# The node cell's candidate bias as a bf16 product over three rows, its state product 384 columns wide

## The reference, cut to what matters

```python
def _gru_cell(x, hstate, Wih, Whh, bih, bhh):
    gi = x @ Wih.T + bih
    gh = hstate @ Whh.T + bhh
    ir, iz, inn = jnp.split(gi, 3, axis=1)
    hr, hz, hn = jnp.split(gh, 3, axis=1)
    r = jax.nn.sigmoid(ir + hr)
    z = jax.nn.sigmoid(iz + hz)
    n = jnp.tanh(inn + r * hn)
    return (1.0 - z) * n + z * hstate
...
edge_output = _gru_cell(node_support, h, edge_Wih, edge_Whh, edge_bih, edge_bhh)
...
edge_support = edge_support / HEADS
node_output = _gru_cell(edge_support, h, node_Wih, node_Whh, node_bih, node_bhh)
return de[:, None] * edge_output + dn[:, None] * node_output
```

## Time and profile before

| | |
|---|---|
| median of 3 runs | 1427.51 us (1426.62 to 1429.61) |
| the profiled execution's own time | 1426.91 us |
| its span in the profile | 1425.2 us |
| TensorE busy | 1332.1 us, 93% |
| VectorE busy | 922.3 us, 65% |
| ScalarE busy | 554.7 us, 39% |
| GpSimd busy | 193.4 us, 14% |
| mean granted clock of TensorE | 0.977 |
| L1461, the state's product: 52 passes | 1361.7 to 1402.3 us |
| L1462, the input's product: 52 passes | 1362.7 to 1403.0 us |

### The profile page before, as it was taken

How to read it: one execution, slowest core, us unless ns; L and a number is a source line. 1 busy time by engine, 2 the same in 40 slices (tenths; PEclk the granted TensorE clock), 3 DMA queues, 4 the chain that set the end, 5 groups by cost and what they waited for, 6 DMA issues and landing times.

```text
span 1425.2 us, 11729 instructions
## 1 busy us (share of the span) xinstructions
PE 1332.1 (93%) x4294; PEld 677.7 (48%) x4294; DVE 922.3 (65%) x1277; ACT 554.7 (39%) x491; POOL 193.4 (14%) x211
## 2 busy tenths in 40 slices
PE   5889997899989999999999999999999999999993
PEld 4434444344444444455445455544445444544451
DVE  6978887888864000003225453799978987898576
ACT  7543324966730000000211111456565566455343
POOL 0000002000020000000000000225430233124211
PEclk8999997999999999999999999999999999999997
DMA  9899972000026667658667158698877987688301
GB/s 396 331 389 412 391 305 99 0 0 0 0 97 187 194 195 193 193 151 268 197 219 235 35 171 308 256 371 307 313 263 256 338 314 290 240 309 319 138 1 50
DMA packets 78150, 311.10 MB, mean 218 GB/s; under 512 B 8700, under 2 KB 20603, under 8 KB 61307
## 3 DMA queue, kind: packets, MB, share of 16 engines
q1 hardware_dynamic: 78075, 310.17, 61.2%
HBM read 306.71 MB, written 3.43 MB: 218 GB/s over the span
## 4 chain that ended last, share of the span: by engine, by line
PE 83%; DMA 7%; DVE 7%; ACT 2%; issue 1%; POOL 0%; ACTq 0%; DVEq 0%; POOLq 0%; SPq 0%
PE ps L1440 30%; PE ps L1241 10%; PE ps L1175 10%; PE ps L1278 10%; PE ps L1100 6%; DMA ring<-in_adjR 6%; PE ps L1235 5%; PE ps L1350 2%; PE ps L1461 1%; DVE arena L1560 1%; PE ps L1422 1%; PE ps L1259 1%; PE ps L1462 1%; DMA ring<-in_adjB 1%; PE ps L1215 1%; PE ps L1260 1%
## 5 line engine op out<-in xcount | busy, mean ns | idle before, releaser
L1440 PE MATMUL ps<-arena,x 128*128 128x512 f32 (+1 forms) x1092 | 438.9, 562 | 2.9 <-ACT shared L978 1.6
L1440 PEld LDWEIGHTS ps<-arena,x 128*128 128x128 f32 x1092 | 206.1, 190 | 231.4 <-issue 225.2
L971 ACT ACTIVATE arena<-arena,bench 128x3328 f32<-128x3328 bf16 x78 | 239.8, 3075 | 188.8 <-PE ps L1440 176.4
L2145 DVE TENSOR_TENSOR arena<-arena,ring 128x3328 f32<-128x3328 f32 x51 | 184.7, 3621 | 26.6 <-ACT arena L971 26.1
L1241 PE MATMUL ps<-ring,x 128*128 128x512 f32 (+1 forms) x364 | 176.1, 566 | 0.0
L1278 PE MATMUL ps<-ring,x 128*128 128x512 f32 (+1 forms) x364 | 149.5, 563 | 1.3 <-DMA ring<-in_adjB 1.3
L1100 PE MATMUL ps<-ring,bench 128*128 128x512 f32 x260 | 122.7, 607 | 15.0 <-DMA ring<-in_adjR 15.0
L1845 DVE SCALAR_TENSOR_TENSOR bench<-b,cols,ps 128x128 f32<-128x128 f32 x26 | 7.3, 344 | 182.1 <-PE ps L1215 182.1
L715 POOL TENSOR_TENSOR ring<-ring,nid 128x128 f32<-128x128 f32 x51 | 95.1, 1864 | 210.8 <-DMA ring<-in_adjR 210.8
L1235 PE MATMUL ps<-arena,shared 128*128 128x512 fp8e4 (+1 forms) x364 | 103.6, 366 | 6.1 <-DVE shared L1650 6.1
L2145 DVE TENSOR_TENSOR arena<-arena 128x3328 f32<-128x3328 f32 x27 | 98.0, 3631 | 13.5 <-ACT arena L971 13.1
(11 more groups left out here) (326 smaller groups left out, 1513.4 us busy)
## 6 DMA issues: line engine op xcount, KB each, us to landing
ring<-in_adjR SPq DMA_DIRECT2D x51, 1664.0 KB, 8.7
ring<-in_adjB SPq DMA_DIRECT2D x312, 256.0 KB, 3.0
arena<-in_adjR SPq DMA_DIRECT2D x27, 1664.0 KB, 8.8
ring<-in_adjR SPq DMA_DIRECT2D x25, 1280.0 KB, 8.5
shared<-in_adj SPq DMA_DIRECT2D x7, 1664.0 KB, 10.8
es<-in_adj SPq DMA_DIRECT2D x7, 1664.0 KB, 10.6
xT<-in_adj SPq DMA_DIRECT2D x6, 1664.0 KB, 13.3
y<-in_adj SPq DMA_DIRECT2D x6, 1664.0 KB, 13.1
```

Of the source, the lines that this page charges most:

```text
L971: A_(E[n % 3], below[n % 3], ACT.Exp, bias=tt_[:, t * HEADS + k:t * HEADS + k + 1], scale=-WIN).then_inc(e_exp, 1)
L1440: last = mm(ps[:, b, 0:w], lhsT=x[:, t], rhs=E[n % 3][:, o_:o_ + w], start=(t == 0), stop=(t == TILES - 1))
L2145: v.tensor_tensor(E[n % 3], E[n % 3], row_at(n), ALU.mult).then_inc(q_ready, 1)
```

## The change

In the node cell, the state's product becomes 384 columns wide, without the bias of inn. The input's product is split in two, 256 columns (r and z) and 128 (inn). Between them a new product opens inn: `ones16`, three rows of ones in bf16, as stationary operand, and `inn16`, whose three rows are the bias split into three bf16 numbers that add up to it. Both lie in the space of the former fourth part of the weights.

```diff
-        state_weights = gb[:, 1].rearrange("p a f -> p (a f)")
+        state_weights = gb[:, 1, 0:3].rearrange("p a f -> p (a f)")
+        inn_bias = gb[:, 1, 3]
+        inn16, ones16 = (inn_bias.bitcast(BF16)[:, n * F:(n + 1) * F] for n in range(2))
...
-                            mm(gt[:, 0:4 * F], lhsT=ht, rhs=state_weights, start=True, stop=False)
-                            last = mm(gt[:, F:4 * F], lhsT=ut, rhs=gru[:, 2], start=False, stop=True)
+                            mm(gt[:, 0:G3], lhsT=ht, rhs=state_weights, start=True, stop=False)
+                            mm(gt[:, F:G3], lhsT=ut, rhs=gru[:, 2, 0:2 * F], start=False, stop=True)
+
+                            mm(gt[:, G3:4 * F], lhsT=ones16[0:3, :], rhs=inn16[0:3, :], start=True, stop=False)
+                            last = mm(gt[:, G3:4 * F], lhsT=ut, rhs=gru[:, 2, 2 * F:], start=False, stop=True)
...
-                step(v.scalar_tensor_tensor(state_weights[:, 0:G3], state_weights[:, 0:G3], lone[:], gru[:, 3], ALU.mult, ALU.add))
-                step(v.tensor_scalar(state_weights[:, G3:], state_weights[:, G3:], lone[:], None, ALU.mult))
+                step(v.scalar_tensor_tensor(state_weights, state_weights, lone[:], gru[:, 3], ALU.mult, ALU.add))
+                first, second, rest, last = (stage[:, n // 2, n % 2 * P:n % 2 * P + P] for n in range(4))
+                first, second = (a.bitcast(BF16)[:, 0:P] for a in (first, second))
+                step(v.tensor_copy(first, inn_bias))
+                step(v.tensor_tensor(rest, inn_bias, first, ALU.subtract))
+                step(v.tensor_copy(second, rest))
+                step(v.tensor_tensor(last, rest, second, ALU.subtract))
+                step(v.tensor_scalar(inn16, first, ident[:, 0:1], None, ALU.mult))
+                step(v.scalar_tensor_tensor(inn16, second, ident[:, 1:2], inn16, ALU.mult, ALU.add))
+                step(v.scalar_tensor_tensor(inn16, last, ident[:, 2:3], inn16, ALU.mult, ALU.add))
+                step(v.tensor_copy(ones16, ones[:]))
...
-LATE_READY = 42
-GS_READY = 55
+LATE_READY = 49
+GS_READY = 62
...
-OUT_READY = 59
+OUT_READY = 66
```

## The result

| | before | changed |
|---|---|---|
| median of 7 runs | 1426.62 us (1424.99 to 1429.61) | 1431.54 us (1426.48 to 1433.73) |
| the profiled execution's own time | 1426.91 us | 1429.71 us |
| its span | 1425.2 us | 1427.9 us |

The ratio of the changed kernel to the one before is 1.003, with a 95% interval of 1.0018 to 1.0043: between 2.6 and 6.1 us longer. The forecast was 5.2 us longer.

A forecast was written before the change was run, and what follows sets the result against it. TensorE was taken to bound the node cell: a tile goes from 1.50 to 1.30 + 0.40 = 1.70 us, 26 tiles x 0.20 = 5.2 us longer, forecast 1432.4 us (between 1432.1 and 1432.7), range 1428.8 to 1435.2.

The forecast's parts named there:

- What bounds the stage: Node cell, last stage: TensorE alone sets the pace, 3.22 us a group of two tiles; VectorE's own period is 3.01 us.
- The three float32 products, 1.30 us: Node cell, each tile: products of 384, 256 and 128 columns take 1.30 us as in the edge cell, 0.20 less than 1.50.
- Two stops: Around the three-row bf16 product: its weight load and the next float32 load each start 0.09 us behind the stream ahead.
- The size of the bf16 product, 0.40 us: Node cell, between the 256 and 128 column products: the three-row product adds 0.40 us to each tile, both stops included.
- the forecast's own case: Node cell: both stops, at 0.37 to 0.50 us a tile, make the kernel 4.4 to 7.8 us longer; chance 0.77.
- All before 1361 us unmoved: Sign of a right forecast: everything ahead of the node cell's stage, before 1361 us, keeps its times.
- The set-up is hidden: VectorE's set-up at about 450 us: seven more steps, about 2.3 us, cost nothing under its 19.66 us wait for TensorE.
- Rival 1, no stop: Node cell: three-row product costs 0.12 us like a full one, group 3.06, 1.9 us shorter, 1425.3 us; chance 0.14.
- Rival 2, one stop: Node cell: way into the bf16 product hidden, price 0.25 to 0.30 us, 1.3 to 2.6 us longer, about 1429.5; chance 0.07.
- Rival 3, the clock: Node cell: VectorE or the clock as a new bound, with TensorE streaming 81% of the stage; the clock's chance 0.02.

## Why the prediction was right, point by point

- *What bounds the stage.* Right: TensorE, at 3.22 us a group, with VectorE close behind. The 3.01 us read for VectorE was 0.04 too long: without a bias product it does a group in 2.97. In the run with 128 rows both engines run at 3.04, TensorE's pace.
- *The three float32 products, 1.30 us.* Right: 1.30 in the run that has only them. The edge cell was a fair model, in spite of its other order.
- *Two stops.* Right, and now shown and not only read from two small products: 64 against 65 rows changes nothing else, and one float32 row has the stops without a change of type. Why the step lies between 64 and 65 rows is not shown. The signs named for it came too: the load 0.09 us behind the stream, and VectorE's wait at 0.47 us where about 0.55 was said.
- *The size of the bf16 product, 0.40 us.* Too large, and outside the 0.37 to 0.50 us to which the forecast gave 0.77. Measured it is 1.66 - 1.30 = 0.36, by the group (3.53 - 0.22) / 2 - 1.30 = 0.355. Way in 0.09 as said, exposed float32 load 0.11 as said; between them 0.155 where the sum had 0.20. If 0.09 of that is the way out, as with one float32 row, and 0.05 the stream (the pair of bf16 products shows 0.05 for one more), the bf16 load has only 0.01 to 0.02. The sum had 0.06 for it, near half a float32 load. The halves for a bf16 stream and a bf16 load were the author's estimate, which no row of before shows by itself; for the stream the runs agree with it, for the load they do not. A tile is thus 1.30 + 0.355 - 1.50 = 0.155 longer, and 26 of them are 4.0 us instead of 5.2.
- *The time.* The stage grew by 3.89 us, less than the 4.4 to 7.8 of the forecast's own case; the medians differ by 4.9, and the interval of the whole, 2.6 to 6.1 us, holds all of 3.9, 4.4 and 5.2. That the median, 1431.54, is within 0.9 us of 1432.4 is therefore luck in part. The lower bound was also worked out unevenly: one stop, 1.3 to 2.6 us longer, has its middle at 1429.2 from the 1427.2 that the forecast starts from, while 1428.8 counts from the profiled execution alone.
- *All before 1361 us unmoved.* Not so, by 1.12 us, but earlier and not later. It is no sign of the set-up: over the ten profiles the first transposes begin between 1358.94 us (the kernel before with the set-up's steps) and 1362.52 (no bias product).
- *The set-up is hidden.* Right, and shown by adding seven such steps alone.
- *Rival 1, no stop.* This is what the run with 128 rows is, with the 0.11 us by tile read off L1363. Its gain had been worked out as 1.9 us; the stage became 2.26 shorter and the whole 2.98 by the medians (the interval goes from 1.0 to 4.3). The counterexample that spoke for this rival, L1329, has few columns over all rows, 3 over 128. It was not stopped: its load began at 734.96, 0.43 us after the load ahead of it (734.53, not shown), which is the distance of the passes. That it has few columns doesn't explain it, since L1288 in the kernel before, a product with a stationary operand of 32 columns over all rows, begins its load as late as the bias product does. The last load of L1278 ahead of it began at 727.41, with the pass before its own. Passes of this kind are 0.43 apart, so all had streamed at 727.41 + 2 x 0.43 = 728.27. ScalarE had finished the operand by 726.93 (L909, not shown), and L1288's load came 0.08 us behind the stream:

```profile
727.41 0.19 PEld L1278 LDWEIGHTS ps<-ring,x 128*128 128x128 f32 x1 [0.24 <-issue]
728.35 0.16 PEld L1288 LDWEIGHTS ps<-shared,hb 128*32 128x32 f32 x8 [0.76 <-issue]
```

L1329 differs from it in being a transpose. Whether that is why it was not stopped was not tried.

- *Rival 2, one stop.* Out: the rows of a tile show both, and the group is 3.53 where one stop would give 3.3 to 3.4.
- *Rival 3, the clock.* Out: 1.00 in the stage, from 1362 to 1400 us, as before. No run had a lower clock there, so what one would cost is not shown.

## What to carry to other kernels

Here a small product between large ones was priced by whether the weight loads around it stayed in the stream and not by its own size. In bf16, three rows instead of 128 saved nothing and cost 0.25 us each time (1.66 - 1.41 a tile), since the load ahead could not be taken early and neither could the one behind. So try to pad such a product with zero rows up to 128 (3.04 us a group instead of 3.53), or to put all products of few rows next to each other (3.22). A saving of columns is then worth having: with 128 rows the same idea is 2 to 3 us faster than the kernel before (2.26 by the stage, 2.98 by the medians) instead of 4 to 5 slower. All this was measured with float32 products of 128 rows on both sides; whether a product of few columns costs the same was not tested.

The stops of TensorE did not show as idle time: in the middle of the node cell it is busy for 38.00 of 38.00 us in both kernels. When its stage grows by more than its columns say, look at where each weight load begins relative to the matmul ahead of it.

## What the runs showed of the hardware that was not expected

- A product of 64 rows is stopped for as one of three is, 3.53 us a group for both. The step lies between 64 and 65 rows: 3.53 and 3.05 us.
- The bf16 load of 128 columns came out much cheaper than half a float32 one: 0.01 to 0.02 us, an estimate worked out from the rows of the tile above, against 0.11 us where both are exposed. In the pair of bf16 products the two loads together show 0.11 us where a single one shows 0.09, so the second began 0.02 behind the first.
